# ScalarE's weighing of the two tiles that GpSimd joins, between the last near outputs in place of behind them

## The chip, the cores and the metric

One Trainium2 chip, one NeuronCore of it. The metric is the device time of one execution in microseconds (us). The kernel before took 886.15 us, the median of three runs (886.14 to 887.43).

## What is computed

One AdaLN block on x of shape 2 x 1024 x 256, all float32. Causal attention with 16 heads comes first, and behind it a mixture of 8 experts, of which each row uses its best two:

```python
h = _layernorm(x) * (1 + ca) + sa
x = x + ga * attn(h)                       # 16 heads, causal
h = _layernorm(x) * (1 + cb) + sb
top_vals, top_idx = top_k(h @ gate_w.T, 2)
w = softmax(top_vals)
y_all = h @ expert_w + expert_b            # 8 experts
x = x + gb * sum_f(w[f] * y_all[top_idx[f]])
```

The rows are held as 16 tiles of 128 rows: 8 tiles of batch 0, and of batch 1 four "near" ones (tiles 8 to 11) and four "late" ones (12 to 15).

## The kernel before, in words

Each engine runs one instruction stream, written out by hand, and the engines are joined by semaphores. An engine that waits holds up all that stands behind the wait on it.

The attention fills the first 800 us. The expert part behind it works in three ways:

- **Batch 0.** The rows are sorted by expert into slots of 128 rows (`SLOTS`, 23 of them). TensorE multiplies each slot by its expert's weights, ScalarE copies the output from PSUM to `y_slot` (`slot_finish`, L1621 to L1626), and SyncE stores that to DRAM (L579).
- **Near tiles.** The same with 15 more slots (`SLOTS1`). Their outputs are the "near outputs". `slot_product` (L1335) is TensorE's part, `store_slot` (L605) SyncE's. A ring of 8 buffers holds `y_slot`, each with a semaphore `y_stored`.
- **Late tiles.** TensorE computes all 8 experts for each of the four tiles d = 0 to 3 (`experts`, L1394). ScalarE (`mix_first`) and VectorE (`mix`, L2351) add them up by weight, and `finish` (L2333 to L2337) makes the output rows.

For batch 0 and the near tiles each row's two expert outputs are fetched back from DRAM into `picked` by indirect DMAs that GpSimd issues (`gather(j)`, L919, two for each tile j). Five semaphores `gathered` are used in turn. Then tile j is *joined*: w0 * first + w1 * second, times gb, plus the residual. ScalarE's `weigh(j, f)` (L1671 to L1676) scales one of the two by its weight. For ten of the twelve tiles VectorE does the rest (`join_part`, L2362, L2365, L2368), weighing the second itself, so ScalarE weighs the first alone. For tiles 6 and 7 (`POOL_JOINS`) ScalarE weighs both, and GpSimd adds, scales and adds the residual (`pool_join`, L927, L929, L932).

GpSimd's stream at the end is: gathers of tiles 0 to 7, `pool_join(6)`, `pool_join(7)`, gathers of tiles 8 to 11. `gather(8)`, the first of the near tiles, waits until all near outputs are stored (`y_stored`, L913).

ScalarE's stream in the near slots is: for each slot s the copy of slot s + 2's turned rows (`slot_upper`), the finish of slot s - 1, and now and then a `weigh`. Behind the loop stand the finish of the last slot (number 37), the four weighs of tiles 6 and 7, `hidden2_hi(3)`, `mix_first(2)`, and the near tiles' weighs. VectorE's last stretch is `mix(2)`, `finish(2)`, `join(8)`, `mix(3)` with `join(9)` and `join(10)` inside it, `finish(3)`, `join(11)`; SyncE stores each result.

Every `weigh` with f = 0 waits for both gathers of its tile:

```python
def weigh(j, f=0):
    if f == 0:
        act.wait_ge(gathered[j % GATHERS], 32 * (j // GATHERS + 1))
```

Of the kernel before, what the change touches and what calls it, by code (L numbers as in the profile page):

```python
# [47 lines left out]
FREE = 2  # L48
# [6 lines left out]
HALF = NT // 2  # L55
SLOTS = FREE * NT + EXPERTS - 1
SLOTS1 = FREE * HALF + EXPERTS - 1
ALL_SLOTS = SLOTS + SLOTS1
# [7 lines left out]
POOL_JOINS = (6, 7)  # L66
# [65 lines left out]
def joins_by(i):  # L132

    return max(0, min(JOIN_OPS * (NT - len(POOL_JOINS)), 4 * i // 3))
# [21 lines left out]
def adaln_block(nc, x, wq, bq, wkv, bkv, wo, gate_w, expert_w, expert_b, c_in, wmod, out):  # L156
    ctx = ExitStack()
    with ctx:
# [261 lines left out]
        def slot_bank(s):  # L420

            return kv_bank(s % 2) if s < SLOTS else (ps_o, ps_m)[s % 2]
# [54 lines left out]
        vector_joins = [j for j in range(JOINS) if j not in POOL_JOINS]  # L477
        weighs = [(j, f) for j in range(JOINS) for f in range(FREE if j in POOL_JOINS else 1)]
# [970 lines left out]
        def _(act):  # L1449
# [163 lines left out]
            def slot_upper(s):  # L1613

                act.wait_ge(slot_t, s + 1)
                if s >= SLOT_PLANES:
                    act.wait_ge(slot_mm, s - SLOT_PLANES + 1)
                keep_hi(slot_hi[s % SLOT_PLANES][:, :, :].rearrange("p k t -> p (k t)"),
                        slot_turned(s)[:, 0:KE * P]).then_inc(slot_hi_set, 1)

            def slot_finish(s):  # L1621

                act.wait_ge(slot_mm, s + 1)
                if s >= SLOT_OUT:
                    act.wait_ge(y_stored[s % SLOT_OUT], 16 * (s // SLOT_OUT))
                nc.scalar.activation(y_slot[:, s % SLOT_OUT, :], slot_bank(s)[:, 0:O], ACT.Copy).then_inc(slot_out, 1)  # L1626
# [9 lines left out]
            def hidden2_hi(d):  # L1636

                act.wait_ge(late_read, HALF + d + 1)
                if d >= 2:
                    act.wait_ge(moe_mm, (d - 1) * 4)  # L1640
                keep_hi(h2_hi[d % 2][:, :, :], h2[:, d, :, :]).then_inc(h2_hi_set, 1)
# [29 lines left out]
# [4 lines that stand above are left out]
                w = (r_weight if j < NT else near["weight"])[:, f, j % NT:j % NT + 1]  # L1675
                nc.scalar.activation(picked[:, f, j, :], picked[:, f, j, :], ACT.Identity, scale=w).then_inc(weighed, 1)  # L1676
# [64 lines left out]
            for s in range(SLOTS, ALL_SLOTS):  # L1741
                if s + 2 < ALL_SLOTS:
                    slot_upper(s + 2)
                if s > SLOTS:
                    slot_finish(s - 1)
                for o in range(joins_by(s - SLOTS), joins_by(s - SLOTS + 1)):
                    if o % JOIN_OPS == 0:
                        weigh(o // JOIN_OPS)
            slot_finish(ALL_SLOTS - 1)
            for j, f in weighs[len(vector_joins) - HALF:len(vector_joins) - HALF + FREE * len(POOL_JOINS)]:  # L1750
                weigh(j, f)
            hidden2_hi(3)
            mix_first(2)
            weigh(NT)
# [710 lines left out]
```

## Time and profile before

| | us |
|---|---|
| median of the three runs | 886.15 |
| lowest and highest | 886.14, 887.43 |
| the profiled execution's own time | 888.38 |
| its span, first to last instruction | 886.6 |
| TensorE busy in the span | 865.9 (98%) |
| VectorE busy | 744.0 (84%) |
| ScalarE busy | 542.8 (61%) |
| GpSimd busy | 330.2 (37%) |

The span is 1.78 us shorter than the profiled execution's own time, which lies 2.23 us above the median. Times of rows are microseconds from the start of the span. The busy share is an average over stages with different limits. The stage of this change is the last 26 us of the span; from 863.2 to 877.5 us TensorE is busy throughout, and from 877.5 us on it has nothing left to do.

### The profile page before, as it was taken

The page shows a single profiled execution, that of the slowest core. Times are in us where ns is not written, and L with a number is a line of the kernel's source. Part 1 is how long each engine was busy: PE and PEld are TensorE (multiplying, and loading weights), DVE is VectorE, ACT ScalarE, POOL GpSimd, SP SyncE. Part 2 cuts the span into 40 slices and gives each one's busy share as a digit, 9 for nine tenths or more (in the row PEclk, how much of TensorE's full clock was granted, in tenths as well). Part 3 has the DMA queues.
Part 4 walks back from the last instruction along what each step waited for, and adds up shares of the span by engine and source line. Part 5 has one row for each costly group of instructions (what it writes and reads, how often), then busy time and mean ns, then how long its engine had stood idle before and what let it go on. Part 6 is the DMA issues. An engine that isn't in the chain of part 4 may idle for free.

```text
span 886.6 us, 17025 instructions
## 1 busy us (share of the span) xinstructions
PE 865.9 (98%) x5433; PEld 772.0 (87%) x5433; DVE 744.0 (84%) x1684; ACT 542.8 (61%) x1249; POOL 330.2 (37%) x400
## 2 busy tenths in 40 slices
PE   8999999999999999999999999999999999999995
PEld 7788888888888888888888989999898888889994
DVE  6877888888888888878878888888888989888777
ACT  4687666666666666664566666666666666665462
POOL 3654122222222222131434444444422223587465
PEclk9999999999999999999999999999999999999998
DMA  7000710000000000200000000000000000442493
GB/s 268 1 12 14 248 50 13 13 12 12 12 12 12 12 12 12 100 15 6 1 26 13 14 13 13 13 13 13 13 13 13 11 9 11 146 164 75 146 288 114
DMA packets 37203, 43.35 MB, mean 49 GB/s; under 512 B 3105, under 2 KB 34367, under 8 KB 37055
## 3 DMA queue, kind: packets, MB, share of 16 engines
q1 hardware_dynamic: 34776, 36.20, 12.7%
q0 software_dynamic: 2304, 6.29, 2.3%
q8 instruction: 36, 0.59, 0.3%
q14 instruction: 31, 0.25, 0.1%
q10 hardware_dynamic: 56, 0.02, 0.0%
HBM read 32.28 MB, written 15.20 MB: 54 GB/s over the span
## 4 chain that ended last, share of the span: by engine, by line
PE 89%; DVE 5%; POOL 2%; ACT 1%; issue 1%; DMA 1%; POOLq 0%; SPq 0%; DVEq 0%; ACTq 0%
PE ps_t L1093 14%; PE ps_s L977 8%; PE ps_s L981 8%; PE ps_s L978 8%; PE ps_o L969 7%; PE ps_o L973 7%; PE ps_o L970 7%; PE ps_m L977 4%; PE ps_m L981 4%; PE ps_m L978 4%; PE ps_m L969 3%; PE ps_m L973 3%; PE ps_m L970 3%; PE ps_o L1103 1%; PE ps_t L977 1%
## 5 line engine op out<-in xcount | busy, mean ns | idle before, releaser
L1451 ACT ACTIVATE pt_hi<-ps_t 128x512 fp32r<-128x512 f32 (+2 forms) x320 | 171.0, 534 | 124.9 <-PE ps_t L1093 124.2
L1501 ACT ACTIVATE probs<-ps_s,neg_max 128x128 f32<-128x128 f32 (+7 forms) x256 | 190.1, 742 | 79.7 <-DVE neg_max L1890 76.9
L1899 DVE TENSOR_TENSOR pt_lo<-ps_t,pt_hi 128x512 fp32r<-128x512 f32 (+2 forms) x320 | 192.6, 602 | 12.8 <-ACT pt_hi L1451 9.0
L1890 DVE TENSOR_REDUCE neg_max<-ps_s 128x1 f32<-128x128 f32 (+7 forms) x256 | 192.6, 752 | 3.7
L725 POOL TENSOR_TENSOR q_lo<-raw,q_hi 128x512 fp32r<-128x512 f32 x60 | 77.3, 1289 | 310.5 <-ACT q_hi L1451 310.5
L1093 PE MATMUL ps_t<-ident,probs 128*128 128x128 f32 x1152 | 188.6, 272 | 0.9 <-DVE pt_lo L1899 0.9
L1093 PEld LDWEIGHTS ps_t<-ident,probs 128*128 128x128 f32 x1152 | 141.9, 141 | 20.9 <-DVE pt_lo L1899 4.9
L977 PE MATMUL ps_s<-k_hi,q_hi 128*128 128x512 f32 (+2 forms) x354 | 148.6, 420 | 2.4 <-ACT probs L1501 2.4
L1937 DVE SCALAR_TENSOR_TENSOR acc<-ps_m,rsum,acc 128x256 f32<-128x256 f32 x256 | 111.5, 477 | 16.4 <-PE ps_m L981 15.7
L1884 DVE TENSOR_TENSOR ps_s<-ps_s,mask 128x128 f32<-128x128 f32 x256 | 75.7, 296 | 57.2 <-PE ps_s L981 49.6
L981 PE MATMUL ps_s<-k_hi,q_lo 128*128 128x512 f32 (+2 forms) x354 | 123.4, 349 | 0.0
L978 PE MATMUL ps_s<-k_lo,q_hi 128*128 128x512 f32 (+2 forms) x354 | 122.8, 347 | 0.0
L969 PE MATMUL ps_o<-pt_hi,v_hi 128*128 128x512 f32 (+2 forms) x320 | 119.6, 374 | 0.7 <-DVE o_lo L1904 0.7
L973 PE MATMUL ps_o<-pt_lo,v_hi 128*128 128x512 f32 (+2 forms) x320 | 115.5, 361 | 0.0
L970 PE MATMUL ps_o<-pt_hi,v_lo 128*128 128x512 f32 (+2 forms) x320 | 115.2, 360 | 0.0
L977 PEld LDWEIGHTS ps_s<-k_hi,q_hi 128*128 128x128 f32 x354 | 66.9, 189 | 8.0 <-issue 2.4
L977 PE MATMUL ps_m<-wo_hi,o_hi 128*128 128x256 f32 x256 | 72.7, 284 | 0.1
L981 PEld LDWEIGHTS ps_s<-k_hi,q_lo 128*128 128x128 f32 x354 | 66.5, 188 | 6.8
L981 PE MATMUL ps_m<-wo_hi,o_lo 128*128 128x256 f32 x256 | 72.3, 282 | 0.0
L978 PE MATMUL ps_m<-wo_lo,o_hi 128*128 128x256 f32 x256 | 72.1, 282 | 0.0
L978 PEld LDWEIGHTS ps_s<-k_lo,q_hi 128*128 128x128 f32 x354 | 67.7, 191 | 2.0
L973 PEld LDWEIGHTS ps_o<-pt_lo,v_hi 128*128 128x128 f32 x320 | 60.1, 188 | 8.4
(340 smaller groups left out, 1725.2 us busy)
## 6 DMA issues: line engine op xcount, KB each, us to landing
slot_out_dram<-y_slot SPq DMA_DIRECT2D x38, 128.0 KB, 2.8
wq_raw<-in_L_attn_wq_dram SPq DMA_DIRECT2D x32, 128.0 KB, 2.4
wo_raw<-in_L_attn_wo_dram SPq DMA_DIRECT2D x32, 128.0 KB, 2.0
wkv_raw<-in_L_attn_wkv_dram SPq DMA_DIRECT2D x2, 1024.0 KB, 6.4
acc<-in_L_attn_x_dram SPq DMA_DIRECT2D x2, 1024.0 KB, 17.0
we_raw<-in_L_ffn_expert_w_dram SPq DMA_DIRECT2D x1, 2048.0 KB, 8.6
slot_rows<-slot_rows_dram SPq DMA_DIRECT2D x2, 1024.0 KB, 8.5
slot_rows_dram<-in_L_attn_x_dram SPq DMA_DIRECT2D x1, 1920.0 KB, 16.9
```

What stands on the lines that cost most here:

```text
L969: nc.tensor.matmul(out_ap, a[0], b[0], start=start, stop=False)
L970: nc.tensor.matmul(out_ap, a[1], b[0], start=False, stop=False)
L973: return nc.tensor.matmul(out_ap, a[0], b[1], start=False, stop=stop)
L977: nc.tensor.matmul(out_ap, a[0], b[0], start=start, stop=False)
L978: nc.tensor.matmul(out_ap, a[0], b[1], start=False, stop=False)
L981: return nc.tensor.matmul(out_ap, a[1], b[0], start=False, stop=stop)
L1093: last = pe.transpose(ps_t[:, q % 2, col:col + P], probs[par][:, p0:p0 + P], ident[:, :])
L1451: return nc.scalar.activation(dst, src, ACT.Copy, scale=scale)
L1501: nc.scalar.activation(probs[par][:, prob_offset(i):prob_offset(i) + w], ps_s[:, i % 2, col:col + w], ACT.Exp, bias=neg_max[:, par, i:i + ...
L1890: nc.vector.tensor_reduce(neg_max[:, par, i:i + 1], ps_s[:, i % 2, col:col + w], AXIS_X, ALU.max, negate=True).then_inc(max_set, 1)
L1899: nc.vector.tensor_tensor(pt_lo[:, q % PT, lo:CH], ps_t[:, q % 2, lo:CH], pt_hi[:, q % PT, lo:CH].bitcast(F32), ALU.subtract).then_inc(pt_ ...
L1937: last = nc.vector.scalar_tensor_tensor(row, ps_m[:, i * E:(i + 1) * E], rsum[:, par, tile:tile + 1], row, ALU.mult, ALU.add)
```

## The change

The four weighs of tiles 6 and 7 stand elsewhere in ScalarE's stream. Slots are numbered 0 to 37 (`ALL_SLOTS` is 38). The two weighs of tile 6 follow the finish of slot 35 and precede that of slot 36. The first weigh of tile 7 stands between the finishes of slots 36 and 37, and its second behind that of slot 37. Their number, their operands and their count on the semaphore `weighed` stay; no other engine's stream is changed.

```diff
                 for o in range(joins_by(s - SLOTS), joins_by(s - SLOTS + 1)):
                     if o % JOIN_OPS == 0:
                         weigh(o // JOIN_OPS)
+                if s + 2 == ALL_SLOTS:
+                    weigh(POOL_JOINS[0], 0)
+                    weigh(POOL_JOINS[0], 1)
+            weigh(POOL_JOINS[1], 0)
             slot_finish(ALL_SLOTS - 1)
-            for j, f in weighs[len(vector_joins) - HALF:len(vector_joins) - HALF + FREE * len(POOL_JOINS)]:
-                weigh(j, f)
+            weigh(POOL_JOINS[1], 1)
             hidden2_hi(3)
             mix_first(2)
             weigh(NT)
```

On ScalarE, around the last three finishes (`y_slot`; `ps_m` and `ps_o` are the two PSUM banks that the slots use in turn; `picked` rows are weighs):

```order
 L1626 ACTIVATE y_slot_160<-ps_o 128x256
 L1626 ACTIVATE y_slot_160<-ps_m 128x256
+L1676 ACTIVATE picked_153<-picked_153,r_weight_132 128x256 x2
 L1626 ACTIVATE y_slot_160<-ps_o 128x256
+L1676 ACTIVATE picked_153<-picked_153,r_weight_132 128x256
 L1626 ACTIVATE y_slot_160<-ps_m 128x256
-L1676 ACTIVATE picked_153<-picked_153,r_weight_132 128x256 x4
+L1676 ACTIVATE picked_153<-picked_153,r_weight_132 128x256
 L1451 ACTIVATE h2_hi1_209<-h2_207 128x256
```

The row of four has come apart: two weighs stand two finishes earlier, one stands one finish earlier, and one stays where it was.

On GpSimd, from the joins of tiles 6 and 7 to the gathers of tile 9, with what each instruction waits for:

```order
L927 TENSOR_TENSOR picked<-picked 128x256 [waits weighed]
L929 TENSOR_TENSOR picked<-picked,mod_rows_116 128x256 [waits rows_step]
L932 TENSOR_TENSOR picked<-picked,acc 128x256 [waits rows_step]
L927 TENSOR_TENSOR picked<-picked 128x256 [waits weighed]
L929 TENSOR_TENSOR picked<-picked,mod_rows_116 128x256 [waits rows_step]
L932 TENSOR_TENSOR picked<-picked,acc 128x256 [waits rows_step]
L919 DMA picked<-slot_out_dram,n_place_u 128x256 [waits y_stored5,y_stored4,y_stored6,y_stored3,y_stored7,y_stored2,gathered3,y_stored1,y_stored0]
L919 DMA picked<-slot_out_dram,n_place_u 128x256
L919 DMA picked<-slot_out_dram,n_place_u 128x256 [waits gathered4]
```

Nothing moved here: this is the stream of both kernels.

## Rows read from the trace of the kernel before

**Rows 1.** The page, chain that ended last: shares of the span by engine
```profile
PE 89%; DVE 5%; POOL 2%; ACT 1%; issue 1%; DMA 1%; POOLq 0%; SPq 0%; DVEq 0%; ACTq 0%
```
**Rows 2.** The same chain in order of time, its last part: start us, us, what
```profile
876.16 2.86 DMA picked<-slot_out_dram,n_place_u
...
884.04 0.43 DVE picked L2368
```
**Rows 3.** Timeline of GpSimd, 856 to 870: start us, us, instruction, [idle before <-releaser]
```profile
856.20 0.95 POOL L919 DMA_INDIRECT picked<-slot_out_dram,r_place_u  x1 [0.30 <-issue]
...
858.94 0.95 POOL L919 DMA_INDIRECT picked<-slot_out_dram,r_place_u  x1 [0.30 <-issue]
864.50 0.74 POOL L927 TENSOR_TENSOR picked<-picked 128x256 f32<-128x256 f32 x1 [4.61 <-ACT picked L1676]
...
866.89 0.92 POOL L927 TENSOR_TENSOR picked<-picked 128x256 f32<-128x256 f32 x1
...
868.76 0.80 POOL L932 TENSOR_TENSOR picked<-picked,acc 128x256 f32<-128x256 f32 x1
869.73 0.98 POOL L919 DMA_INDIRECT picked<-slot_out_dram,n_place_u  x1 [0.17 <-issue]
```
**Rows 4.** Timeline of ScalarE, 861 to 865
```profile
861.34 0.38 ACT L1626 ACTIVATE y_slot<-ps_m 128x256 f32<-128x256 f32 x1 [0.21 <-PE ps_m L981]
862.39 0.38 ACT L1626 ACTIVATE y_slot<-ps_o 128x256 f32<-128x256 f32 x1 [0.67 <-PE ps_o L981]
863.23 0.38 ACT L1626 ACTIVATE y_slot<-ps_m 128x256 f32<-128x256 f32 x1 [0.46 <-PE ps_m L981]
863.51 1.70 ACT L1676 ACTIVATE picked<-picked,r_weight 128x256 f32<-128x256 f32 x4
```
**Rows 5.** Tile picked, 855 to 889: landing of all its DMAs
```profile
DMA to landing us min/median/max: 2.9/3.3/4.6
```
**Rows 6.** L919, tile 7's second gather, issued at 858.94: landing
```profile
DMA to landing us min/median/max: 4.3/4.3/4.3
```
**Rows 7.** SyncE's store of slot 37: its timeline row, then landing
```profile
863.64 0.32 SPq L605 DMA_DIRECT2D slot_out_dram<-y_slot  x1
...
DMA to landing us min/median/max: 3.0/3.0/3.0
```
**Rows 8.** L605, all eleven near stores from 853.6 on: landing
```profile
DMA to landing us min/median/max: 2.7/3.2/3.9
```
**Rows 9.** Batch 0's last store (L579), its landing, and GpSimd's first gather behind it
```profile
L579 SPq DMA_DIRECT2D slot_out_dram<-y_slot x1: 768/768/768, 835.9 to 835.9; - x1
...
DMA to landing us min/median/max: 2.9/2.9/2.9
...
839.67 0.99 POOL L919 DMA_INDIRECT picked<-slot_out_dram,r_place_u  x1 [1.31 <-DMA slot_out_dram<-y_slot]
```
**Rows 10.** Timeline of VectorE, 865 to 880
```profile
865.76 0.57 DVE L2333 TENSOR_TENSOR y_sum<-y_even,y_odd 128x256 f32<-128x256 f32 x1
866.37 0.84 DVE L2335 TENSOR_TENSOR y_sum<-y_sum,mod_rows 128x256 f32<-128x256 f32 x1
...
872.11 0.42 DVE L2333 TENSOR_TENSOR y_sum<-y_even,y_odd 128x256 f32<-128x256 f32 x1
...
873.02 0.42 DVE L2337 TENSOR_TENSOR y_sum<-y_sum,acc 128x256 f32<-128x256 f32 x1
874.47 0.49 DVE L2362 SCALAR_TENSOR_TENSOR picked<-picked,near_weight 128x256 f32<-128x256 f32 x1 [1.03 <-ACT picked L1676]
...
875.46 0.42 DVE L2368 TENSOR_TENSOR picked<-picked,acc 128x256 f32<-128x256 f32 x1
875.80 0.48 DVE L2351 SCALAR_TENSOR_TENSOR y_even<-ps_s,coef,y_even 128x256 f32<-128x256 f32 x1
...
877.00 0.49 DVE L2362 SCALAR_TENSOR_TENSOR picked<-picked,near_weight 128x256 f32<-128x256 f32 x1 [0.33 <-ACT picked L1676]
...
879.59 0.48 DVE L2362 SCALAR_TENSOR_TENSOR picked<-picked,near_weight 128x256 f32<-128x256 f32 x1 [0.40 <-ACT picked L1676]
```

## Prediction

> **What bounds the kernel now.** I read the page's chain first. TensorE holds 89% of it and GpSimd 2% [rows 1], which says only that the long attention part is TensorE's. The change sits in the last 26 us, so I read the chain in order of time there. TensorE leaves it at slot 37's product. From then on it runs ScalarE's finish of slot 37, two weighs of tile 6, GpSimd's two joins, the near gathers one behind the other, the landing of tile 10's second gather (issued at 876.16, landed 2.86 us later, at 879.02), then VectorE to the last residual at 884.04 [rows 2]. What ends last in this stage is therefore the near gathers, and what holds those is GpSimd: it stood idle for 4.61 us until ScalarE had weighed tile 6, joined from 864.50 to 869.56, and issued the first near gather at 869.73, 0.17 us later [rows 3].
>
> ScalarE itself waited for slots while this went on. Before the finishes of slots 36 and 37 it was idle for 0.67 and 0.46 us [rows 4]. Two weighs fit in the first of these gaps almost whole: from one finish or weigh to the next the timeline shows a pitch of 0.28 us (863.23 to 863.51), and four weighs in 1.70 us, of some 0.50 us each, have a pitch of 0.40.
>
> **The change part by part.** No instruction is added or removed; four are moved, and they issue nothing else. The sum is made against the profiled execution and then carried to the median.
>
> *Tile 6's weighs.* They need both gathers of tile 6. The second was issued at 856.20 [rows 3], and the longest landing of any DMA of this tile was 4.6 us [rows 5], so the data are there by 860.8. The weighs start 0.28 us behind the finish at 861.34, at 861.62 and 862.02, and end at 862.53. Slot 36's finish moves from 862.39 to 862.42 (862.02 + 0.40); I cost that at nothing, since slot 37's finish is later in any case and the stores of both go out in turn. Before, GpSimd began 0.08 us behind the second weigh (863.51 + 0.40 + 0.51 = 864.42, then 864.50). Now it begins at 862.61, which is **1.89 us earlier**.
>
> *Tile 7's first weigh.* This is the one place where the change adds a wait. Tile 7's second gather was issued at 858.94 and took 4.3 us [rows 3, 6], so it landed at 863.24. Queued behind this wait on ScalarE are slot 37's finish, tile 7's second weigh, the cut of the last late tile and its first two mixes. Slot 37 was ready at 863.23 [rows 4]. Now the weigh goes at 863.26 and the finish 0.40 us behind it, at 863.66: **0.43 us late**. The late tile's cut and mixes keep slack, since TensorE has its earlier tiles to do, and I cost them at nothing; without that cover the cost is again 0.4 us at the most.
>
> *Slot 37's store.* It was issued at 863.64 and took 3.0 us [rows 7], landing at 866.64, so GpSimd, busy until 869.56, never waited for it. Now it is issued at 864.07 and lands at 867.07. The near gathers wait for it. What such a wait costs when it does end last is shown once, at batch 0: the last store was issued at 835.9, landed 2.9 us later, at 838.8, and the first gather began at 839.67, that is 0.85 us behind [rows 9]. By that the near gathers can begin at 867.07 + 0.85 = **867.92**.
>
> *GpSimd's joins.* From 862.61 they take 2.39 us for tile 6 (864.50 to 866.89) and 2.84 us for tile 7 with what follows (866.89 to 869.73) [rows 3]. Tile 7's second weigh ends at 864.5, before it is wanted. This gives 867.84 for the first gather, if the second join again meets VectorE's output sums. The lower bound is two joins of 2.39 us, 867.56 with the 0.17 us. So the join path and the store path end within 0.1 us of each other, and the wait for the stores, which ended last nowhere near here before, now ends last. I take the later: 867.92 for 869.73 before, a gain of **1.81 us**.
>
> *From the gathers to the end.* The gathers are issued at their own pace, so all landings move by 1.81 us. VectorE must be able to follow. It stood idle for 1.03, 0.33 and 0.40 us before the joins of tiles 8, 9 and 10 [rows 10], 1.76 us together; and where it has no wait it starts 0.08 us before the last one ends (875.46 + 0.42 against 875.80), which makes up to 0.24 us more. VectorE's own floor is thus a gain of about 2.0 us: `finish(2)` holds it until 873.44, and `finish(2)` hangs on TensorE, which does not move. The gathers' 1.81 is the smaller, so tile 10's join, 879.59 before, stands at 877.8, and what is behind it follows unchanged.
>
> *Sum.* 1.81 us, from 888.38 to 886.6 for the profiled execution. The median of the runs lies 2.23 us lower, at 886.15, and loses the same: **884.35 us**. About 0.2% (1.77 us) is what a measurement of this kernel can tell from no change, and this forecast lies on that line.
>
> **A rule against the change.** In the timeline, VectorE's sums over two SBUF tiles take 0.57 and 0.84 us beside GpSimd's joins, and 0.42 us alone [rows 10], so the two engines do hold each other up; GpSimd's own operation was 0.92 us where the first was 0.74 [rows 3]. The Trainium skill (SBUF — State Buffer, Who interferes with whom) says that a VectorE instruction with two SBUF inputs contends with a GpSimd instruction that reads SBUF, and that the side which issues first keeps the shared port while the other is blocked outright. By that rule each of tile 7's three operations could be put off by a whole VectorE operation. The trace so far agrees on the contention, and shows most of the delay on VectorE's side.
>
> **The rivals.**
> 1. *VectorE's floor.* The store lands in 2.7 us, the least seen [rows 8], and the joins meet no sum. The gathers then start at 867.6, 2.1 us earlier, and VectorE's floor caps the gain at 2.0: 884.2 us. For it: 3.0 us is near the low end. Against it: both paths must be quick. Chance 0.13.
> 2. *Slot 37's store lands late.* At 3.9 us, as the slowest of the eleven [rows 8], the gathers start at 868.82 and the gain is 0.91 us: 885.25 us. For it: the new order puts it 0.43 us nearer to the other stores. Against it: the transfers had thinned out by then, and this store took 3.0. Chance 0.12.
> 3. *The joins are stretched.* Each of tile 7's three operations waits for a whole sum of 0.42 us: 2.39 + 1.26 = 3.65 us from 865.00, so the gathers start at 868.82 and the gain is 0.91 us, again 885.25 us. Against it: with just such sums beside it, tile 7's join took 2.84 us to the gather. Chance 0.07. This is what the rule above would make of it.
> 4. *Slower: tile 7's gather holds slot 37's finish.* The place is the new wait. From the landing to the first near gather there are 4.68 us (867.92 less 863.24). The gain is gone when that gather lands at 865.05, 6.1 us after its issue, and the kernel is slower by more than the measurement's grain from 866.8 on, 7.9 us after its issue; at 8.0 us it is 888.0 us. For it: it is the slow end of a crowded queue. Against it: no landing above 4.6 us there [rows 5]. Chance 0.05.
> 5. *No change.* Something else, which the chain doesn't show because it was covered, holds the near gathers at their old time: 886.15 us. Against it: every semaphore that they wait for is accounted for above. Chance 0.03.
>
> **How the numbers follow.** The forecast has 0.60. Its own spread, from the pitches' rounding and a store landing 0.3 us either way, is 884.0 to 884.7, and I put 0.37 of it beyond the 0.2% line and 0.23 within. Faster: 0.37 + 0.13 = 0.50. Within 0.2%: 0.23 + 0.12 + 0.07 + 0.03 = 0.45. Slower: 0.05. The range reaches from just past VectorE's floor (883.9) over rivals 2 and 3 to 885.5, and leaves out rivals 4 and 5 and some noise.
>
> **What would show it.** In the changed kernel's profile two weighs should stand between the finishes at 861.3 and 862.4, GpSimd's first join should start at 862.6, slot 37's finish at 863.7 behind a weigh that waited for a DMA, and the first near gather at 867.9 with a releaser "DMA slot_out_dram<-y_slot". VectorE's idle before joins 8 and 9 should be gone and some 0.2 us be left before join 10. A first near gather before 867.5, or one with no wait on the stores, would show the store step wrong; a finish of slot 37 later than 864.5 would bear out rival 4; sums and joins that overlap at over 1 us each, rival 3. If the gathers move by 1.8 us and the end does not, VectorE's floor was read wrongly.

## The result, and the profile after

The changed kernel took **884.28 us**, the median of nine runs (883.86 to 886.02), beside 886.17 us for the kernel before, also nine runs (886.01 to 888.26). The ratio is 0.9973, with an interval of 0.9965 to 0.9982: a gain of about a quarter of a percent, small but clear of the noise. The two medians differ by 1.89 us. The ratio says 0.5 us more than that, because four of the nine runs of before lay at 887.4 to 888.3 and one run of after at 886.02, the others of each close together. Like against like, the gain is 1.9 us.

| | before | after |
|---|---|---|
| median of the runs, us | 886.17 | 884.28 |
| profiled execution, us | 888.38 | 884.22 |
| its span, us | 886.6 | 882.5 |
| mean granted clock | 0.995 | 0.998 |

The two profiled executions differ by 4.1 us, more than the change can claim: slot 37's product ended at 863.19 us before and ends at 861.04 after, so 2.15 us were there before the changed place is reached. Part of it shows at the very start. Of each kernel the timeline in windows gives, for 10 to 20 us: us, busy time and instructions of TensorE, weight load, VectorE, ScalarE and GpSimd, granted clock, DMA share, GB/s. First before:

```profile
10.00:20.00 10.00, 8.40 (x44) 6.86 (x44) 6.00 (x14) 7.30 (x12) 5.08 (x5) 0.83 0.91 309
```

and after:

```profile
10.00:20.00 10.00, 8.29 (x49) 6.67 (x49) 7.36 (x16) 8.61 (x15) 5.19 (x5) 1.00 0.91 305
```

The granted clock was 0.83 in one and 1.00 in the other, and five matmuls fewer were begun. That is a difference between executions and not between the kernels: the kernel before shows 0.83 there once more (e2) and 1.00 another time (e15). From here on I count from the end of slot 37's product, written "+1.31" for 1.31 us behind it. That end is 863.19 in the rows of before and 861.04 in those of after.

The page's chain that ended last, by engine, of after:

```profile
PE 91%; DVE 6%; ACT 1%; issue 1%; POOL 0%; DMA 0%; SPq 0%; ACTq 0%; DVEq 0%; POOLq 0%
```

GpSimd's 2% and the 1% of a DMA are gone from it [rows 1], and VectorE has one more. The chain now goes from TensorE's products of the third late tile straight to VectorE's mix of them at 869.04, and stays on VectorE to the end.

ScalarE's timeline of after (start us, us, instruction, [idle before <-releaser]):

```profile
859.18 0.39 ACT L1626 ACTIVATE y_slot<-ps_m 128x256 f32<-128x256 f32 x1 [0.20 <-PE ps_m L981]
859.46 0.90 ACT L1676 ACTIVATE picked<-picked,r_weight 128x256 f32<-128x256 f32 x2
860.26 0.37 ACT L1626 ACTIVATE y_slot<-ps_o 128x256 f32<-128x256 f32 x1
860.52 0.50 ACT L1676 ACTIVATE picked<-picked,r_weight 128x256 f32<-128x256 f32 x1
861.08 0.38 ACT L1626 ACTIVATE y_slot<-ps_m 128x256 f32<-128x256 f32 x1
861.36 0.50 ACT L1676 ACTIVATE picked<-picked,r_weight 128x256 f32<-128x256 f32 x1
```

The finishes of slots 36 and 37 no longer have idle time before them, where they had 0.67 and 0.46 us [rows 4], and yet slot 37's finish is not late: +0.04 as before (863.23 less 863.19, 861.08 less 861.04). Tile 7's first weigh, at 860.52, waited for nothing.

GpSimd's timeline of after:

```profile
860.44 0.74 POOL L927 TENSOR_TENSOR picked<-picked 128x256 f32<-128x256 f32 x1 [3.58 <-ACT picked L1676]
...
862.77 0.74 POOL L927 TENSOR_TENSOR picked<-picked 128x256 f32<-128x256 f32 x1
...
864.41 0.80 POOL L932 TENSOR_TENSOR picked<-picked,acc 128x256 f32<-128x256 f32 x1
865.38 0.98 POOL L919 DMA_INDIRECT picked<-slot_out_dram,n_place_u  x1 [0.17 <-issue]
```

The first join begins at -0.60 instead of +1.31, 1.91 us earlier. The first near gather follows the joins by the same 0.17 us as before [rows 3], at +4.34 instead of +6.54: 2.20 us earlier, and not held by a store.

VectorE's timeline of after. From the sums of the third late tile to the end no idle time stands in it:

```profile
863.61 1.01 DVE L2336 TENSOR_TENSOR y_sum<-y_even,y_odd 128x256 f32<-128x256 f32 x1
864.65 0.85 DVE L2338 TENSOR_TENSOR y_sum<-y_sum,mod_rows 128x256 f32<-128x256 f32 x1
...
870.91 0.42 DVE L2340 TENSOR_TENSOR y_sum<-y_sum,acc 128x256 f32<-128x256 f32 x1
871.25 0.48 DVE L2365 SCALAR_TENSOR_TENSOR picked<-picked,near_weight 128x256 f32<-128x256 f32 x1
...
873.36 0.48 DVE L2365 SCALAR_TENSOR_TENSOR picked<-picked,near_weight 128x256 f32<-128x256 f32 x1
...
875.46 0.47 DVE L2365 SCALAR_TENSOR_TENSOR picked<-picked,near_weight 128x256 f32<-128x256 f32 x1
...
879.91 0.42 DVE L2371 TENSOR_TENSOR picked<-picked,acc 128x256 f32<-128x256 f32 x1
```

The three idle times before the joins [rows 10] are gone. VectorE ends at +19.29 (880.33 less 861.04) where it ended at +21.28 (884.47 less 863.19): a gain of 1.99 us behind slot 37, and this is the gain of the medians.

### The profile page after: what moved, and what is told of

Read it like the earlier page. It is cut to its first block, busy times and chain, and to the rows that moved or that the text cites. A ratio compares the mean times of both kernels' runs of the same rounds, so it can differ in the third digit from the quotient of the medians.

```text
span 882.5 us, 17025 instructions
## 1 busy us (share of the span) xinstructions
PE 863.4 (98%) x5433; PEld 769.9 (87%) x5433; DVE 741.8 (84%) x1684; ACT 542.3 (61%) x1249; POOL 328.8 (37%) x400
## 3 DMA queue, kind: packets, MB, share of 16 engines
q1 hardware_dynamic: 34776, 36.20, 12.7%
## 4 chain that ended last, share of the span: by engine, by line
PE 91%; DVE 6%; ACT 1%; issue 1%; POOL 0%; DMA 0%; SPq 0%; ACTq 0%; DVEq 0%; POOLq 0%
PE ps_t L1093 14%; PE ps_s L977 9%; PE ps_s L981 8%; PE ps_s L978 8%; PE ps_o L969 7%; PE ps_o L973 7%; PE ps_o L970 7%; PE ps_m L977 4%; PE ps_m L981 4%; PE ps_m L978 4%; PE ps_m L969 3%; PE ps_m L973 3%; PE ps_m L970 3%; PE ps_o L1103 1%; PE ps_t L977 1%
## 5 line engine op out<-in xcount | busy, mean ns | idle before, releaser
L1940 DVE SCALAR_TENSOR_TENSOR acc<-ps_m,rsum,acc 128x256 f32<-128x256 f32 x256 | 111.3, 476 | 16.4 <-PE ps_m L981 15.8
```

The source lines that it names most:

```text
L1940: last = nc.vector.scalar_tensor_tensor(row, ps_m[:, i * E:(i + 1) * E], rsum[:, par, tile:tile + 1], row, ALU.mult, ALU.add)
```

## The experiments

The theory after the result: the weighs put the joins 1.9 us earlier, the joins put the gathers 2.2 us earlier, and VectorE, without idle time left, passes only 2.0 us of that on to the end. The rivals: slot 37's store bounds the gathers after all; the joins are stretched by VectorE; the gain lies in how the executions fell, not in the order.

All experiments ran on other chips than the first. There the kernel before itself takes 910 to 912 us. The windows of two 45 us stretches, columns as above, show why; first of before on the first chip:

```profile
820.00:865.00 45.00, 44.69 (x320) 41.42 (x320) 32.32 (x130) 24.43 (x74) 24.49 (x26) 1.00 0.68 217
```

and the same kernel again, as e2:

```profile
830.00:875.00 45.00, 27.46 (x150) 24.17 (x149) 16.78 (x63) 10.17 (x30) 23.00 (x24) 0.81 0.45 143
```

TensorE is busy for 27.46 of 45 us instead of 44.69. The longest pause in e2, 9.93 us, is put down to "issue", that is, to nothing that the profile shows, and another, of 5.04 us, to ScalarE. ScalarE itself stood still for 10.95 and 5.82 us at about the same times, by the releaser "remote", one that the profile does not know. Such pauses are in both kernels, lie ahead of the changed place, and by the times add some 24 us to both. What comes behind slot 37 can still be compared, with one difference: by then GpSimd has long issued tile 7's last gather (20.0 us ahead of the end of slot 37's product in e2, against 4.25 in before), so on these chips no weigh had to wait for a gather of tiles 6 and 7. The table holds what each profile shows there, counted from the end of slot 37's product; "mix 4" is the start of VectorE's mix of expert 4 of the last late tile, and the last column the idle time in front of it. The ratio is to the kernel before on the same chip.

| kernel | median us | ratio and interval | finish 37 | first join | first near gather | mix 4 | VectorE's end | idle before mix 4 |
|---|---|---|---|---|---|---|---|---|
| before | 886.17 | | +0.04 | +1.31 | +6.54 | +15.13 | +21.28 | none |
| after | 884.28 | 0.9973 (0.9965 to 0.9982) | +0.04 | -0.60 | +4.34 | +13.63 | +19.29 | none |
| e1, the change | 911.97 | 0.9998 (0.9989 to 1.0007) | +0.04 | -0.61 | +4.31 | +15.82 | +21.48 | 2.13 |
| e2, before | 912.17 | 1.0001 (0.9991 to 1.0010) | +0.04 | +1.31 | +6.54 | +15.15 | +21.23 | none |
| e3, tile 6 only | 912.95 | 0.9998 (0.9986 to 1.0010) | +0.04 | -0.59 | +4.63 | +16.15 | +21.80 | 2.48 |
| e4, all four between | 911.27 | 0.9982 (0.9972 to 0.9991) | +1.08 | +0.46 | +5.64 | +14.46 | +20.54 | none |
| e5, tile 7 earlier | 910.07 | 1.0002 (0.9993 to 1.0010) | +0.04 | -0.64 | +4.54 | +13.60 | +19.55 | none |
| e6, less of GpSimd | 909.87 | 0.9999 (0.9989 to 1.0009) | +0.04 | -0.61 | +4.03 | +15.44 | +21.10 | 1.77 |
| e7, less of VectorE | 910.07 | 0.9995 (0.9984 to 1.0006) | +0.03 | -0.61 | +4.33 | +15.73 | +21.40 | 2.09 |
| e8, less of both | 909.80 | 0.9997 (0.9987 to 1.0008) | +0.04 | -0.62 | +4.28 | +15.67 | +21.33 | 2.06 |
| e9, VectorE padded | 909.87 | 0.9992 (0.9981 to 1.0003) | +0.04 | -0.60 | +4.63 | +14.55 | +20.21 | 0.89 |
| e10, before, padded | 910.80 | 1.0002 (0.9992 to 1.0011) | +0.04 | +1.30 | +6.54 | +15.28 | +21.28 | none |
| e11, ScalarE padded | 910.20 | 0.9999 (0.9989 to 1.0009) | +0.04 | -0.62 | +4.32 | +15.71 | +21.37 | 2.02 |
| e12, the change | 910.25 | 0.9996 (0.9987 to 1.0006) | +0.04 | -0.62 | +4.46 | +14.41 | +20.07 | none |
| e13, mixes first | 912.20 | 1.0003 (0.9994 to 1.0013) | +0.04 | -0.64 | +4.43 | +14.43 | +21.40 | 2.08 |
| e14, stores later | 911.80 | 1.0004 (0.9994 to 1.0013) | +0.04 | -0.61 | +4.33 | +15.78 | +21.44 | 2.06 |
| e15, before | 912.33 | 1.0006 (0.9996 to 1.0016) | +0.04 | +1.30 | +6.55 | +15.15 | +21.34 | none |
| e16, the change | 912.34 | 1.0005 (0.9994 to 1.0015) | +0.04 | -0.62 | +4.31 | +15.77 | +21.43 | 2.07 |
| e17, marks | 912.04, one run | | +0.04 | -0.63 | +4.31 | +15.78 | +21.43 | 2.08 |
| e18, marks, mixes first | 914.14, one run | | +0.04 | -0.62 | +4.32 | +15.83 | +22.80 | 3.44 |

### The change and its parts (e1 to e4, one chip)

e1 is the changed kernel, e2 the kernel before.

> The change once more, in five rounds beside the kernel before. Theory A (VectorE's floor): the gain is 1.98 us whatever the start of the run did, so a ratio of 0.9978 between runs of like start, and in the profile VectorE without any idle from its second finish to the end. Theory B (the prediction: slot 37's store sets the near gathers): 1.8 us, ratio 0.9980, and some 0.2 us of idle before tile 10's join. Theory C (the first measurement's 0.9973 is all from the change): 2.4 us again, with the first near gather over 2.4 us nearer to slot 37's product than before.

> The kernel before, unchanged, measured against itself: ratio 1.000. Its profile gives a second sight of what varies from one execution to the next. If the 2.16 us by which the changed kernel's profile stood ahead already before its slots come from TensorE's clock in the first 20 us, this profile shows either a clock of 1.00 there and a span near 884.4 us, or 0.9 and 886.6 us. The distance from slot 37's product to the end should be 21.4 us as before (from 863.08 to 884.47) in both theories; the landing of tile 7's second gather behind slot 37's product may differ by up to 0.9 us.

(The 21.4 us in the second text counts from 863.08, where the chain has TensorE's last piece of slot 37 begin; from its end, as in the table, it is 21.28.) The early steps came out as on the first chip to 0.03 us: join -0.61, gather +4.31. The end did not: VectorE's +21.48 against +21.23, and a ratio of 0.9998. Between the gathers and the end something new took 2.13 us. What the first 20 us cost could not be read from e2: its clock there was 0.83 and its span 911.0 us, neither of the two cases expected.

e3 moves tile 6's weighs only:

```
                     weigh(POOL_JOINS[0], 1)
-            weigh(POOL_JOINS[1], 0)
             slot_finish(ALL_SLOTS - 1)
+            weigh(POOL_JOINS[1], 0)
             weigh(POOL_JOINS[1], 1)
```

> Tile 6's two weighs moved, tile 7's two left behind slot 37's finish, so nothing new waits in front of that finish. Theory B (tile 7's first weigh holds the finish by 0.43 us and the store sets the end): faster than the change by 0.1 to 0.2 us. Theory A (in most executions tile 7's gather has landed by then): equal to the change within 0.1 us, 1.98 us faster than before, since tile 7's weighs end 0.5 us before GpSimd wants them.

Tile 6's weighs alone give the whole advance of the first join (-0.59). The first gather is 0.3 us later than in e1 (+4.63 against +4.31), but not for a late weigh of tile 7: one multiply of GpSimd took longer. The timeline of e3 (GpSimd and VectorE):

```profile
889.83 1.02 POOL L929 TENSOR_TENSOR picked<-picked,mod_rows 128x256 f32<-128x256 f32 x1
889.83 0.42 DVE L2336 TENSOR_TENSOR y_sum<-y_even,y_odd 128x256 f32<-128x256 f32 x1
```

The two operations start together; here VectorE keeps its 0.42 us and GpSimd's takes 1.02 instead of 0.74, where in after VectorE's took 1.01 and GpSimd's 0.74. The same happened in e9 (1.03 us, and again +4.63), which moves tile 7's weigh. So moving that weigh is worth nothing that these profiles or times show.

e4 puts all four weighs between the finishes of slots 36 and 37:

```
-                if s + 2 == ALL_SLOTS:
-                    weigh(POOL_JOINS[0], 0)
-                    weigh(POOL_JOINS[0], 1)
-            weigh(POOL_JOINS[1], 0)
+            for j in POOL_JOINS:
+                weigh(j, 0)
+                weigh(j, 1)
             slot_finish(ALL_SLOTS - 1)
-            weigh(POOL_JOINS[1], 1)
```

> All four weighs between the finishes of slots 36 and 37. Slot 37's finish then waits for four weighs at a pitch of 0.40 us and goes out about 1.0 us late, its store too; GpSimd's first join starts 0.9 us later than in the change. Both theories: first near gather about 0.9 us later than in the change. Theory A: VectorE's floor gives 0.2 us of that back, so 0.7 us slower than the change, a gain of 1.3 us against before. Theory B: 0.9 us slower, a gain of 0.9 us.

ScalarE's timeline of e4:

```profile
885.64 0.39 ACT L1626 ACTIVATE y_slot<-ps_m 128x256 f32<-128x256 f32 x1 [0.18 <-PE ps_m L981]
886.72 0.39 ACT L1626 ACTIVATE y_slot<-ps_o 128x256 f32<-128x256 f32 x1 [0.70 <-PE ps_o L981]
887.00 1.70 ACT L1676 ACTIVATE picked<-picked,r_weight 128x256 f32<-128x256 f32 x4
888.60 0.36 ACT L1626 ACTIVATE y_slot<-ps_m 128x256 f32<-128x256 f32 x1
```

Here the finish of slot 37 is late, by 1.04 us against the others: four weighs do not fit where one does. GpSimd's joins are later by about as much (+0.46 for -0.61), and the near gathers, at +5.64, again stand 0.16 us behind the last join operation: the joins bound them. Slot 37's store, issued at 889.0 and landed 2.0 us later, would have let them go at 891.9 (with the 0.85 us of batch 0); they went at 893.16.

### Gathers, joins and the sums beside them (e5 to e8, a second chip)

e5 puts tile 7's first weigh one finish further forward, next to tile 6's two:

```
                     weigh(POOL_JOINS[0], 1)
-            weigh(POOL_JOINS[1], 0)
+                    weigh(POOL_JOINS[1], 0)
             slot_finish(ALL_SLOTS - 1)
```

> Tile 7's first weigh stands with tile 6's, in front of slot 36's finish, so its wait for the gather now holds two finishes. If that gather lands late as in the trace of before (0.16 us behind the end of slot 37's product), slots 36 and 37 finish 0.9 and 0.4 us late, the first near gather starts within 0.2 us of its place in the change by the store's path (prediction's theory), and the time is that of the change plus 0 to 0.2 us. If it lands early, as the changed kernel's profile suggests, slot 36's finish is at most 0.4 us late and the time is the change's. The rival of a kernel slower than before asks for over 3 us more than the change; neither theory gives that.

Slot 37's finish stayed at +0.04. That does not test the wait that the prediction had there, since tile 7's gathers had been issued some 20 us before. Of the gain behind slot 37, the profile shows 1.7 us (+19.55), the runs none (1.0002). The profiled execution was the fastest of the eleven (908.59 us, the median 910.07), so how the others ended behind slot 37 is not known.

e6 leaves out GpSimd's multiply of tile 7, e7 VectorE's multiply in the join of tile 8, e8 both; else each is the changed kernel, which itself was not run on this chip.

```
-                pool.wait_ge(rows_step, done + 1)
-                pool.tensor_tensor(picked[:, 0, j, :], picked[:, 0, j, :], ..., ALU.mult).then_inc(rows_step, 1)
-                pool.wait_ge(rows_step, done + 2)
+                if j == POOL_JOINS[0]:
...
+                else:
+                    pool.wait_ge(rows_step, done + 1)
```

> The change, with the multiply by gb left out of GpSimd's join of tile 7 (the output of that tile lacks this factor): GpSimd is done 0.8 us earlier. The near gathers then start with slot 37's store, at its landing plus 0.85 us: 0.3 to 0.5 us earlier than in the change. Theory A (VectorE's floor): no gain, the same time as the change within 0.1 us. Theory B (the gathers set the end): 0.3 to 0.5 us faster than the change, or none if the store already set them, and then with a first near gather that waited for a DMA.

> The change, with the multiply by gb left out of VectorE's join of tile 8 (that tile's output lacks this factor): 0.46 us less on VectorE. Theory A: VectorE loses its floor, but tile 10's weigh ends only some 0.1 us before VectorE wants it, so the gain is 0.1 us and idle of 0.3 us appears before tile 10's join. Theory B: no gain at all, since the gathers set the end.

> Both: the multiply by gb left out of GpSimd's join of tile 7 and of VectorE's join of tile 8. Theory A: the two bounds lie within 0.1 us of each other, so only together do they give way: 0.4 us faster than the change. Theory B: as the kernel with less on GpSimd alone.

These were to find which of GpSimd and VectorE sets the end. None moved the time. In all three VectorE stood still for 1.8 to 2.1 us before mix 4 and ended at +21.1 to +21.4, so they do not tell apart what they were made for. That VectorE's floor capped the gain on the first chip therefore rests on the trace of that one execution, in which VectorE has no idle time left. What e6 and e8 do show is what stands behind the joins. GpSimd's timeline of e6, its last join operation and the first near gather:

```profile
890.52 0.74 POOL L935 TENSOR_TENSOR picked<-picked,acc 128x256 f32<-128x256 f32 x1
892.01 0.98 POOL L919 DMA_INDIRECT picked<-slot_out_dram,n_place_u  x1 [0.76 <-issue]
```

With 0.82 us of joining taken away, the gather goes only 0.3 us earlier (+4.03), because GpSimd now waits 0.76 us instead of 0.17. In e8 it waits 1.01 us, and the gather (+4.28) is hardly earlier at all. What it waits for in that place besides its joins is the slots' stores: slot 37's was issued at 888.4 in e6 and landed 2.6 us later, and with the 0.85 us of batch 0 the gather would go at 891.9; it went at 892.01. In e8 the same sum (884.8, 2.8 us) gives 888.5, and it went at 888.59. So the path over the store ends only some 0.05 to 0.3 us before the whole joins would. In three of the profiles in which GpSimd joins early and leaves nothing out it even ended last: e5, e12 and e13 show 0.42, 0.31 and 0.32 us before the first gather (their stores landed after 3.1, 3.0 and 3.0 us), the ten others the 0.16 or 0.17 of joins that end last.

### Does the pause belong to a late block of instructions? (e9 to e12, a third chip)

The pause came before the same instruction each time, which made me think of instructions fetched late. e9 puts 16 memsets of one column on VectorE ahead of the last mixes of the second late tile, which shifts everything behind them by 16 instructions; e10 does so in the kernel before; e11 puts 12 one-column copies on ScalarE; e12 is the change.

```
+            for i in range(16):
+                nc.vector.memset(rsum[:, i // NT, i % NT:i % NT + 1], 0.0)
             mix(1, {}, range(2 * DENSE_EARLY, EXPERTS))
```

> The change, with 16 one-column memsets added to VectorE's stream in its idle time before the last output mixes of late tile 1 (some 1.1 us of work in 2.7 us of idle; they write dead data). In five of the six profiles with early gathers on the two later chips VectorE stood still for 1.8 to 2.5 us in front of one and the same instruction, the mix of expert 4 of late tile 3, 13.7 us behind slot 37's product, though all that it waits for was there. Theory P (supply: a block of VectorE's instructions arrives late, asked for 11 instructions before): the standstill moves 16 instructions forward in the stream, into time in which VectorE waits anyway, so it is gone from the last 12 us, VectorE runs through from its second finish, and the gain over before is 1.7 to 2.0 us on any chip. Theory Q (the standstill belongs to that instruction: a semaphore or bank that it waits for): it stays where it was and the gain stays near 0 on such chips. On a chip without the standstill both give the change's own time.

> The kernel before with the same 16 memsets: the control for them. Both theories: the time of the kernel before within 0.2 us, as its profile there shows no standstill; if the memsets moved some other pause, this run shows by how much.

> The change, with 12 one-column copies added to ScalarE's stream behind the first mixes of late tile 2, in idle time, and VectorE's stream untouched. ScalarE's own fetch of instructions, which the DMA rows show 0.2 to 0.3 us beside VectorE's in the kernels with the standstill and 1.2 us or more apart in the kernel before, comes some 3 us earlier. If the two fetches get in each other's way, the standstill is gone or shorter; if VectorE's fetch alone is slow, it stays at 1.8 to 2.5 us and the gain near 0 on such a chip.

> The change a third time, on the chip of the three above, so that they can be compared. Theory A (VectorE's floor, no standstill on this chip): 1.98 us faster than before. Theory P: that less a standstill of 0 to 2.5 us in front of the mix of expert 4 of late tile 3; the median then lies between 0 and 2 us below before, with the single runs spread over that.

In e9 the pause was shorter, 0.89 us, but still before mix 4, not 16 instructions elsewhere. A pause that belongs to a place in the stream of instructions would have moved. Whether the shift made it shorter is not shown, as without it this chip had both 2.02 us (e11) and none (e12). The padding of ScalarE did not remove the pause (2.02 us), and the padding of before changed nothing there (e10). In e12 there was no pause, but VectorE had already waited 0.69 us for a late gather and came to mix 4 only at +14.41.

### What does VectorE wait for? (e13 to e18)

e13 puts the join of tile 9 behind the mixes of experts 4 and 5, e14 the stores of tiles 9 and 10 behind the last late tile's; e15 is the kernel before and e16 the change.

```
-            mix(3, {3: (NT + 1,), 5: (NT + 2,)})
+            mix(3, {5: (NT + 1, NT + 2)})
```

```
-            for j in range(NT, JOINS - 1):
-                store_joined(j)
+            store_joined(NT)
             store_mixed(3)
-            store_joined(JOINS - 1)
+            for j in range(NT + 1, JOINS):
+                store_joined(j)
```

> The change, with VectorE's join of near tile 9 put behind the mixes of experts 4 and 5 of late tile 3 instead of in front of them; nothing else moves. If the pause waits for something that this mix needs from TensorE (a product that really ends later than its record), it starts 1.35 us earlier, when VectorE comes to the mix at +12.3 us behind slot 37's product, and still ends at +15.7: VectorE's end stays at +21.4. If it belongs to the stretch of time in which it fell (+13.7 to +15.8), VectorE stands still in front of the join that now falls there, not in front of the mix, and the end is the same. If it has to do with the store of tile 9 that is issued when join 9 ends, it moves 0.87 us later with the join. On a chip without pauses the end is as of the change, 19.3 us behind slot 37's product, and the store of tile 9 goes out 0.87 us later, without effect.

> The change, with SyncE's stores of tiles 9 and 10 put behind the store of the last late tile. If the store of tile 9 makes VectorE stand still, there is no pause at +13.7 and VectorE ends at +19.3 us behind slot 37's product; the span gains up to 2 us less what three stores issued together cost at the end (0.33 us of issue each: 0 to 0.7 us). If it has nothing to do with it, the pause stands, and VectorE ends at +21.4.

> The kernel before, unchanged: VectorE's end at +21.2 to +21.3 us behind slot 37's product, as in its three other profiles, no pause, and a time within 0.1% of the kernel before.

> The change, unchanged. On a chip like the first (some 886 us for the kernel before): 1.8 to 2.0 us below it, ratio 0.998, and VectorE ends at +19.3 us. On a chip where the kernel before takes some 910 us: GpSimd's first join at -0.6 us, first near gather at +4.3, and VectorE's end anywhere from +19.3 (no pause) to +21.5 (a pause), the ratio between 0.998 and 1.000.

VectorE's timeline of e16, the join of tile 9 ending and mix 4:

```profile
899.48 0.42 DVE L2371 TENSOR_TENSOR picked<-picked,acc 128x256 f32<-128x256 f32 x1
901.97 0.48 DVE L2354 SCALAR_TENSOR_TENSOR y_even<-ps_s,coef,y_even 128x256 f32<-128x256 f32 x1 [2.07 <-PE ps_s L981]
```

and of e13, where the mix of expert 3 stands before it:

```profile
898.68 0.47 DVE L2354 SCALAR_TENSOR_TENSOR y_odd<-ps_s,coef,y_odd 128x256 f32<-128x256 f32 x1
901.23 0.48 DVE L2354 SCALAR_TENSOR_TENSOR y_even<-ps_s,coef,y_even 128x256 f32<-128x256 f32 x1 [2.08 <-PE ps_s L981]
```

The pause came along with mix 4, to +12.35, and not with the join. So it belongs to that instruction, not to the stretch of time. In e14 the store of tile 9 was gone from there and the pause was the same: the store has nothing to do with it. My number for e13 was wrong, though: I had the pause end at +15.7 if it were TensorE's, and it ended at +14.43.

So the last two kernels mark the place. Two memsets of one column stand before mix 4, and the second takes over its wait for TensorE's product.

```
+                    if d == 3 and e == 4:
+                        nc.vector.memset(rsum[:, 0, 0:1], 0.0)
                     if e % 2 == 0:
                         dve.wait_ge(moe_mm, d * 4 + e // 2 + 1)
+                    if d == 3 and e == 4:
+                        nc.vector.memset(rsum[:, 0, 1:2], 0.0)
```

> The change, with two memsets of one column on VectorE in front of the mix of expert 4 of late tile 3: the first waits for nothing, the second takes over the mix's wait for TensorE's product, and the mix keeps its wait for the mix two before it. If VectorE gets no instruction, the pause of some 2.1 us lies ahead of the first mark. If TensorE's signal comes late, it lies between the first mark and the second. If the mix itself is held (its other wait, or the bank that it reads), it lies behind the second. The two marks cost some 0.1 us each. If the pause is gone (the stream is two instructions longer), VectorE ends at +19.5 us behind slot 37's product.

> The same two marks, in the order of e13 (the mixes of experts 4 and 5 in front of the join of tile 9). VectorE comes to the first mark at +12.35 us behind slot 37's product, and TensorE's product has ended by its record at +12.75. Late instructions: the pause lies ahead of the first mark, to about +14.4. A late signal: between the marks, to +14.4, and with no pause at all the second mark starts at +12.8. Held mix: the second mark starts at +12.8 and the mix at +14.4.

VectorE's timeline of e17:

```profile
899.99 0.42 DVE L2375 TENSOR_TENSOR picked<-picked,acc 128x256 f32<-128x256 f32 x1
900.36 0.06 DVE L2348 MEMSET rsum<- 128x1 f32 x1
902.50 0.48 DVE L2358 SCALAR_TENSOR_TENSOR y_even<-ps_s,coef,y_even 128x256 f32<-128x256 f32 x1 [2.08 <-issue]
902.53 0.06 DVE L2352 MEMSET rsum<- 128x1 f32 x1
```

and of e18, with the mixes first:

```profile
899.79 0.06 DVE L2348 MEMSET rsum<- 128x1 f32 x1
903.29 0.48 DVE L2358 SCALAR_TENSOR_TENSOR y_even<-ps_s,coef,y_even 128x256 f32<-128x256 f32 x1 [3.44 <-issue]
903.32 0.06 DVE L2352 MEMSET rsum<- 128x1 f32 x1
```

The first mark runs at once (900.36, 899.79), the second only with the mix. So VectorE does get its instructions. The pause stands where the wait for TensorE's signal stands, and it ends at +15.8 in both (902.50 less 886.72, 903.29 less 887.46), although VectorE comes 1.3 us earlier in e18. The mix's other wait, for the mix two before it, had been met. But by its records TensorE had ended that product long before. Its timeline in e17 shows the last matmul of that product and the last of all:

```profile
899.05 0.39 PE L981 MATMUL ps_s<-we_hi,h_lo 128*128 128x512 f32 x1
...
900.64 0.39 PE L981 MATMUL ps_s<-we_hi,h_lo 128*128 128x512 f32 x1
```

The product that mix 4 needs was over at 899.44 by its record, or +12.7, and the wait ended 3.1 us later; even TensorE's last matmul ends at +14.3 (901.03). These ends are modelled, as the page says of itself. The Trainium skill (Perfetto Trace Analysis, Summary: the profiler window per engine type) says the same of TensorE, that the end is estimated and the signal's travel is not in it; by that the record cannot show the lateness, and no run here shows whether the signal came late, or came in time and was seen late, nor what made it so.

**What the experiments settle and what they leave open.** Twelve of the fourteen kernels that began the joins early on these chips had the pause (all but e5 and e12), and none of the four that began them later (e2, e4, e10, e15). So the change reaches mix 4 early, and there meets a limit that before never met at +15.1. The marks show that this limit stands at VectorE's wait for TensorE's product; e14 excludes the store, e13 the join, and the marks together with e9 missing instructions. But it is no fixed time at which TensorE gives the product free: TensorE's records lie within 0.02 us of each other in all these profiles, and the kernels without the pause passed the same wait at +15.15 (e2, e15), +14.46 (e4) and +13.60 (e5), where one held until +15.8 would have stopped them. Nor is it a fixed length: 2.08 us in e13 and in e17, 3.44 in e18, 0.89 in e9. Why the wait ends at +15.8 in most, at +14.4 or +14.6 in e13 and e9, and before +13.6 in e5 and in after on the first chip, stays open. Open, too, is what makes the pauses ahead of 875 us on these chips, and whether they have to do with this one.

**Is there a better version?** On the later chips e4 was the only kernel whose ratio lies clear of 1 (0.9982; its median is 0.9 us below e2's). It was measured once, as one of sixteen, so some of that may be chance. Its profile ends 0.7 us earlier than e2's: it reaches mix 4 at +14.46, with no pause. It was not run on the first chip. Its gathers start 1.3 us later than the change's, so where the change has no pause e4 should end later (+20.54 against +19.29); that is argued, not measured.

## Why the prediction was right or wrong

The time came out within 0.07 us of the forecast (884.28 for 884.35) and inside its range. The path that was to lead there did not hold, and that the two agree so closely is luck: by the prediction's own sums the store's path gave a gain of 1.81 us, the joins' path 1.89 and VectorE's floor 2.0, so any of the three would have come out within 0.2 us.

- *Tile 6's weighs*: as predicted. The first join came 1.91 us earlier for 1.89.
- *Tile 7's first weigh waits for its gather, and slot 37's finish is 0.43 us late*: **failed**. The finish was not late in after: 0.00 us for 0.43. (On the later chips it could not be, as said above.) I had carried the gather's issue over from before. But GpSimd's gathers of batch 0 begin behind that batch's last store, and its landing varies. That store (L579), its landing, and GpSimd's first gather behind it, in after:

```profile
L579 SPq DMA_DIRECT2D slot_out_dram<-y_slot x1: 319/319/319, 833.7 to 833.7; - x1
...
DMA to landing us min/median/max: 2.1/2.1/2.1
...
836.71 0.99 POOL L919 DMA_INDIRECT picked<-slot_out_dram,r_place_u  x1 [0.82 <-issue]
```

  In both executions the store was issued at -27.3, but here it landed after 2.1 us, where it took 2.9 before [rows 9]. The first gather stands 0.9 us behind the landing as before, though the row names no DMA as releaser, and begins at -24.33 instead of -23.52. The chain of sixteen gathers behind it is 0.8 us earlier against the slots, and tile 7's second gather, issued at 855.91, had landed when the weigh came at 860.52. That is no effect of the change, but a DMA landing that fell well.
- *Slot 37's store lands at +3.88 and binds the near gathers*: **failed**; this was the binding step. The store's landing in after:

```profile
L605 SPq DMA_DIRECT2D slot_out_dram<-y_slot x1: 319/319/319, 861.5 to 861.5; - x1
...
DMA to landing us min/median/max: 2.5/2.5/2.5
```

  Issued at 861.5 and landed 2.5 us later instead of 3.0 [rows 7], it is there at 864.0. Over all twenty profiles this landing takes 2.0 to 3.3 us. With the 0.85 us that I took from batch 0, the gathers could have gone at 864.85; the joins ended at 865.21. So the joins bound, with 0.4 us to spare where I had the store ahead by 0.1. Two terms of the binding sum were oversized: 0.43 us for the late finish, measured 0, and the landing, 3.0 us for 2.5. That the two paths end close together was right: in e5, e12 and e13 the wait did come up, for 0.25 us at the most.
- *GpSimd's joins take 5.23 us to the gather*: they took 4.94 (860.44 to 865.38). Tile 6's took 2.33 for 2.39 and tile 7's 2.61 for 2.84. The overlap with VectorE's sums did exist, but the delay fell on VectorE: its first sum took 1.01 us and its second 0.85, where alone they take 0.42. The rule that I had set against the change, by which each of GpSimd's operations might lose a whole sum, did not come true in after: GpSimd's lost 0.07 us at the most (0.80 for 0.73). It can go the other way, as e3 and e9 show, where one of GpSimd's lost 0.29 us and VectorE's sum beside it nothing; which of the two loses is not settled by the streams of the two engines, which are the same in e3 and in after.
- *VectorE's floor, 2.0 us*: right, and by the trace of after it is what bound. It was rival 1, with a chance of 0.13, and its outcome was the one that came true: gathers more than 2 us earlier (2.20) and a gain capped at 2.0 (1.99). Of its two conditions the quick store held (2.5 us for 2.7); the joins did meet VectorE's sums, but lost hardly anything by it. Rival 1's time was 884.2, and the forecast of 884.35 differed from it by less than a measurement tells apart; that is why a wrong binding step left the number right. Between the two, the chances should have been nearer to even, since the forecast rested on two landings that were known to 0.5 us and a difference of 0.1 us.
- *Slower or unchanged*: not on the first chip. But rival 5 named the case, a thing that the chain of before does not show because it was covered, and on the later chips something of this kind was found, not at the near gathers but at mix 4. I gave it 0.03, and looked for it among the gathers' semaphores alone.
- *Measuring*: that the forecast lay on the 0.2% line was right: the medians differ by 0.21%.

## What to carry to other kernels

Where two limits end within a few tenths of a microsecond, and both hang on DMA landings that vary by more than that, forecast the time and leave the binding step open; price the next limit behind both, since it caps the gain whatever the order. A work item is put best into idle time that its engine has anyway: three of four weighs went into the 0.67 and 0.46 us before the finishes and left slot 37's finish where it was, while four in one gap (e4) cost 1.04. And a gain of 2 us at the end of a kernel should be looked at on more than one chip: here the same first join, the same to 0.02 us, was worth 1.9 us on one chip and nothing that could be measured on three others.

## What the runs showed of the hardware

- The same program takes 886 us on one chip and 910 to 912 us on four others. The extra 24 us lie between 830 and 875 us. In e2 TensorE stood still there for up to 9.93 us at a time, and its granted clock was 0.81 over these 45 us, a mean between its two levels (1.2 and 2.4 GHz); it was 1.00, the higher one, from 800 to 840 us, and 0.66 from 840 to 850, with a pause of 5.04 us that ends at 842.47.
- VectorE can wait for a product of TensorE 3 us beyond the end that TensorE's record gives (+12.7 by the record in e17, +15.8 by the mark), and in other executions it passes the same wait at +13.6 without stopping (e5, after).
- When GpSimd's and VectorE's operations on SBUF tiles met, mostly VectorE's grew, from 0.42 to 1.01 us, with GpSimd's at 0.74 beside it; in e3 and e9 it was GpSimd's, from 0.74 to 1.02 and 1.03 us, with VectorE's at 0.42.
- A store of 128 KB to DRAM landed after 3.0 and 2.5 us for the same slot in before and after, and after 2.0 to 3.3 us over all twenty profiles, while the two paths of the prediction lay 0.1 us apart.
